# One core, a Flamingo block with a routed FFN: the streamed tile's three loads get a slot each on SP, and the slot tables of all engines are replaced

## What is computed

```
q = x @ Wq; k = ctx @ Wk                      # 4 heads of 32, 1024 context rows
scores = q k^T / sqrt(32)
topv, topi = top_k(scores, 32); probs = softmax(topv)   # scattered back, mean over heads
c_t = attn_mean @ (ctx @ Wv)
x' = layernorm(x) * (1 + scale_in(c_t)) + shift_in(c_t)
y  = s4d(x')                                  # long convolution, by real FFTs of 1024 points
y  = y * (1 + scale_out(c_t)) + shift_out(c_t)
xt = x_text + y; xt = layernorm(xt + gelu(ln(xt) @ W1) @ W2)
x  = x + tanh(g) * xt
x  = x + tanh(g2) * (shared_swiglu(ln(x)) + routed_swiglu(ln(x)))   # top-1 of 8 experts, score a sigmoid
```

## Time and profile before

| what | value |
|---|---|
| median of 3 runs | 1906.59 us (1902.35 to 1912.98) |
| profiled execution, its own time | 1909.8 us |
| span of the profiled execution | 1907.9 us |
| before the first MAX8 | 67.7 us |
| frame 0 | 230.4 us |
| frames 1, 2, 3 (no streamed tiles) | 178.4, 181.1, 180.9 us |
| frames 4, 5, 6, 7 | 202.8, 196.7, 194.8, 183.2 us |
| last MAX8 unit to the first of the 18 last tiles | 176 us (1616 to 1792) |
| the last tiles | about 116 us |
| DVE busy | 1564.8 us, 82% |

### The profile page before, as it was taken

One profiled execution on the slowest core, in us unless ns is written; L12 is line 12 of the kernel. 1 busy time (PEld: TensorE's weight loads), 2 busy tenths in 40 slices (PEclk: granted clock), 3 DMA queues, 4 the chain that ended last, 5 costly groups with the idle time before them and its releaser, 6 DMA issues. The chain is left out here.

```text
span 1907.9 us, 20758 instructions
## 1 busy us (share of the span) xinstructions
PE 1402.2 (73%) x6301; PEld 999.9 (52%) x6301; DVE 1564.8 (82%) x2300; ACT 1039.2 (54%) x2110; POOL 1185.0 (62%) x1293
## 2 busy tenths in 40 slices
...
GB/s 229 53 3 14 20 16 50 23 17 45 50 12 17 56 39 12 25 48 111 89 45 67 116 50 28 78 111 61 23 84 69 66 17 50 140 241 86 73 48 25
DMA packets 99219, 114.77 MB, mean 60 GB/s; under 512 B 18786, under 2 KB 77930, under 8 KB 98964
## 3 DMA queue, kind: packets, MB, share of 16 engines
q1 hardware_dynamic: 86964, 98.87, 17.8%
...
## 5 line engine op out<-in xcount | busy, mean ns | idle before, releaser
L1307 DVE MAX8 R<-ZB 128x8 f32<-128x1024 f32 x384 | 471.0, 1227 | 11.9
L1310 DVE MATCH_REPLACE8 ZB<-R,ZB 128x1024 f32<-128x1024 f32 x384 | 464.1, 1209 | 0.0
L669 POOL TENSOR_TENSOR ZB<-ZB 128x1024 f32<-128x1024 f32 x96 | 231.3, 2409 | 150.7 <-ACT ZB L944 146.5
L947 ACT ACTIVATE R<-PS 128x256 f32<-128x256 f32 (+6 forms) x378 | 160.4, 455 | 187.5 <-PE PS L1877 59.8
L944 ACT ACTIVATE R<-R 128x32 f32<-128x32 f32 (+2 forms) x352 | 95.1, 272 | 291.1 <-DVE R L1307 236.7
L671 POOL TENSOR_TENSOR ZB<-ZB 128x1024 f32<-128x1024 f32 x96 | 227.2, 2367 | 7.5
L1604 PE MATMUL PS<-ZR 97*128 97x512 f32 x128 | 81.4, 636 | 148.1 <-ACT ZB L944 120.0
L1299 DVE MAX8 R<-PS 128x8 f32<-128x1024 f32 x128 | 156.4, 1222 | 4.1 <-PE PS L1605 4.1
L950 ACT ACTIVATE R<-R 128x1 f32<-128x1 f32 (+1 forms) x384 | 141.0, 391 | 27.8 <-POOL R L656 23.5
L1303 DVE MATCH_REPLACE8 ZB<-R,PS 128x1024 f32<-128x1024 f32 x128 | 155.4, 1214 | 0.0
L944 ACT ACTIVATE ZB<-ZB,R 128x1024 f32<-128x1024 f32 x128 | 146.1, 1141 | 14.2 <-DVE ZB L1310 14.1
...
## 6 DMA issues: line engine op xcount, KB each, us to landing
...
ZR<-ZR SPq DMA_DIRECT2D x192, 32.0 KB
...
```

The source lines that it names most:

```text
L669: pool.tensor_tensor(e, e, w, ALU.subtract).then_inc(s.g_att, 1)
L947: return act.activation(o, i, ACT.Copy, **k)
L1307: vec.max(ml[:, 8 * r:8 * r + 8], w).then_inc(s.v_tk, 1)
L1310: vec.match_replace(w, ml[:, 8 * r:8 * r + 8], w, NEG).then_inc(s.v_tk, 1)
```

## The change

`tiles` on SP used to yield once for a tile and now yields three times: before the rows' load, before gate and up, and before down. Other streams of SP can come between. The waits are as they were. All slot tables are replaced with other numbers (`POOL_*`, `ACT_*`, `DVE_*`, `PE_*`, `POST_AT`, `SP_*`); no instruction is added or taken away, apart from the activation-table loads, which follow from ACT's order. Lines after 582 are one or two higher in the changed kernel.

```
-SP_QUERY = (28.1, 29.7, 33.4, 34.3)
-SP_TILE = ((-1.9,), (-0.2,), (2.5,), (56.5,), (71.3,))
+SP_QUERY = (24, 24, 24, 30)
+SP_TILE = ((-9.4, -4.9, -2.9), (-2.9, -2.9, -0.2), (2.5, 8.3, 11), (46.7, 46.7, 77.1), (92.3, 93.8, 97))
...
-PE_TILE = ((18.7, 20.4, 20.8, 25.5), (26.2, 38.3, 40, 42.2), (50.4, 53.2, 53.4, 54.1), (99.3, 101.3, 102.2, 104.1), (104.9,
-           106.9, 112.3, 116.5))
+PE_TILE = ((17.9, 23.9, 23.9, 33.4), (37.3, 40.5, 46.1, 51.7), (51.7, 58, 58.4, 58.8), (85.3, 95, 103.5, 109.1), (109.1,
+           113.2, 114.9, 114.9))
...
                     sp.dma_start(txs[j % 2], xs_d[bass.ds(row, 128), :]).then_inc(s_txs[j % 2], 16)
+                    yield tile_slot(j, SP_TILE, 1)
                     if j:
                         on.wait_ge(*q_run("tile", j - 1, T_UP))
                     for lo, nm in ((0, "gate"), (1024, "up")):
...
+                    yield tile_slot(j, SP_TILE, 2)
                     if j:
                         on.wait_ge(*q_run("tile", j - 1, T_DOWN))
```

More of the change, by code:

```diff
@@ L120 @@
 FILM_IN, DFT, INV, FILM_OUT, TURN, UP, DOWN, TURN2, GATE, RANK, COUNT, SHARED, SH_DOWN, NQ = 0, 4, 8, 10, 14, 16, 24, 28, 30, 31, 32, 33, 41, 45
[L123 to L158, removed]
@@ L159 @@
-ACT_EXP = (11.4, 9.3, 16, 13, 9.6, 10.8, 5.8, 8.2, 13.4, 18.4, 10.8, 10.4, 12.8, 8.8, 14.4, 7.6)
-ACT_REST = (12.5, 12.7, 16.9, 13.9, 10.1, 10.8, 10.4, 8.2, 13.6, 18.4, 11, 10.8, 16.8, 9.4, 15.1, 7.6)
-PE_SCORES = (-0.5, -5.2, -4.8, -3.6, -10.3, -6.8, -6.5, -3.1, -10.3, -2.9, 4.3, 1.2, 2.5, -2.3, -2.3, 0.1)
-PE_TILE = ((18.7, 20.4, 20.8, 25.5), (26.2, 38.3, 40, 42.2), (50.4, 53.2, 53.4, 54.1), (99.3, 101.3, 102.2, 104.1), (104.9,
-           106.9, 112.3, 116.5))
-ACT_TILE = ((28.4, 32.5, 34.6), (37.6, 42.9, 51.3), (52.6, 54.2, 60.8), (96, 101.9, 107.8), (108, 120, 120.9))
@@ L165 @@
[L165 to L178, removed]
@@ L179 @@
-SP_QUERY = (28.1, 29.7, 33.4, 34.3)
-SP_KEYS = (8.8, 4.2, 1.9, 0.2)
-SP_INPUT = (-1.7, -0.3)
-SP_POST = (2.2, 99.6, 100.6, 100.6, 121.9)
-SP_TILE = ((-1.9,), (-0.2,), (2.5,), (56.5,), (71.3,))
+POOL_FILM_IN = (7.4, 7.4, 7.8, 9)
+POOL_FOLD = (10.7,)
+POOL_SPECTRUM = (13.5, 19, 19.4, 19.4)
+POOL_INV = (31.2, 31.2)
+POOL_FILM_OUT = (31.2, 31.5, 31.5, 31.5)
+POOL_ROOT = (40.4, 90.5, 107.2)
+POOL_RESIDUAL = (57, 67.7, 77, 88.8)
+POOL_OUT = (90.5, 90.5, 91.8, 93.8)
+POOL_ROUTE = (117.8, 120.5, 121.6)
@@ new lines @@
+POOL_SH = (133.3, 134, 134.2, 134.5)
+POOL_PREP = (-7.8, 57.5)
+POOL_LOW = (3.4, 11.3, 47.5)
+ACT_FILM_IN = (21.9, 22.8, 23.6, 23.8)
+ACT_INV = (43.6, 49.3)
+ACT_FILM_OUT = (50.9, 50.9, 54.7, 54.8)
+ACT_ROOT = (61.8, 103.1, 112.8)
+ACT_NORM = (63.5, 116.4)
+ACT_TURN = (63.5, 63.5)
+ACT_UP = (71.8, 77.1, 77.1, 77.7, 77.7, 85.9, 87.2, 87.4)
+ACT_DOWN = (92.7, 95, 95, 100.2)
+ACT_OUT = (104.8, 105.5, 106.6, 108.5)
+ACT_TURN2 = (120.8, 120.8)
+ACT_ROUTE = (126.8, 127.6)
+ACT_SILU = (126.8, 134)
+ACT_SH = (137.8, 138.7, 141.3, 145.2)
@@ new lines @@
+DVE_SPECTRUM = (29.3, 30.4, 32.3, 33.5)
+DVE_MOMENTS = (55.6, 98.6, 110.1)
+DVE_ROUTE = (118, 120.2)
+DVE_SH = (126.3, 130.1, 131, 132.3)
+ACT_PREP = (6.4, 10.9, 20.4)
+ACT_QUERY = (22.6, 23.2, 26.6)
+ACT_CONTEXT = (8.3, 48.8)
+ACT_KEY = (18.8, 53)
+ACT_FINISH = ((1.4, 2.2, 11, 18.2), (9.3, 11.8, 17.7, 29.9), (4, 8.4, 18.6, 36.2), (4.9, 4.9, 8, 15.5))
+POOL_SUM = (5.8, -1.1, -3.4, -4.7, -8.6, -0.7, 1.4, -2.2, -1.4, 0.6, 3.1, 2.2, 1.9, 8, 11.3, 4)
+ACT_MAX = (5.2, 6.1, 6.4, 3.1, 10, 7.3, 2.9, 11.8, 10.8, 14.2, 10.3, 11.1, 7.5, 4.2, 17, 9.3)
@@ new lines @@
+ACT_EXP = (11.1, 11.2, 11.1, 4.8, 11.3, 10.4, 12.7, 13.8, 15.1, 16.6, 10.7, 11.7, 9.8, 8.8, 17, 9.3)
+ACT_REST = (12.8, 11.2, 11.1, 10.7, 12, 10.4, 14.7, 13.8, 17.9, 16.9, 10.9, 12.1, 11.2, 12.7, 17, 11.6)
+PE_SCORES = (3.4, -3, -4.1, -9.6, -7.7, -1.6, -4.9, 1.5, -3.7, -1, 0.2, -0.8, -4.2, -6.2, -1.9, -1.2)
+PE_TILE = ((17.9, 23.9, 23.9, 33.4), (37.3, 40.5, 46.1, 51.7), (51.7, 58, 58.4, 58.8), (85.3, 95, 103.5, 109.1), (109.1,
+           113.2, 114.9, 114.9))
+ACT_TILE = ((19.4, 26.1, 35.4), (35.4, 41.6, 58.9), (59.6, 61.4, 66.2), (93.8, 100.4, 105.8), (108.1, 115.6, 121.3))
@@ new lines @@
+DVE_TILE = ((25.2,), (51,), (57.8,), (102.8,), (113.6,))
+POOL_TILE = ((29.3,), (47.7,), (79.2,), (119.7,), (139.7,))
+DVE_CHUNK = ((-24.9, -22.3), (-22.3, -17.5), (29.9, 34.3), (44.4, 45.6), (53.9, 54.7), (68, 70.9), (73.3, 74.3), (86.8, 88))
+POOL_CHUNK = ((-62.7, -45.4, -33.6, -27.6, -7), (-29.1, -1.9, 7.7, 10.9, 11.1), (7.9, 16.5, 18.8, 23.6, 23.6), (22.6, 23.6,
+              31, 40, 43.5), (31, 44.7, 44.7, 52.1, 53.7), (49.1, 56.1, 56.1, 61.4, 62.1), (60.2, 68, 68.5, 68.8, 71.7),
+              (68.5, 82.1, 83.2, 85.6, 85.6))
```

11 lines of the change are left out of this document (added).

## The result

The changed kernel takes 1896.48 us (median of 5; 1892.5 to 1898.18) against 1906.59: ratio 0.9941, 95% interval 0.9916 to 0.9966. That is faster, by 0.6%, and inside the range; but the forecast was 32 us and the gain is 10. The profiled execution has a span of 1894.6 us, against 1907.9.

The account below looks back on a forecast made before the run. DVE was taken to bound frames up to 3; in frames 4 to 7 it waits, chiefly for late queries and POOL's order. Terms 26 - 1 + 10 + 2 + 3 - 5 - 3 = 32 us gave 1875 us, range 1856 to 1901.

Parts of the forecast that it names:

- Part 1: Frames 4 to 6: queries sent ahead of the last tile's loads; 26 us gained, 1 us lost to late keys.
- the chain's 38.8 us: DVE's waits at frames' ends, in frames 4 to 7; forecast to fall to 12.4 us, a gain of 26.4.
- rival A: At the last tile, another wait replaces the queries' and 15 to 26 us come back: 1890 to 1901 us; chance 0.15.
- the cover: Time between the previous tile's down load and the keys' DMAs at the key copy; forecast only some 9 us.
- Part 2: Frame starts: POOL's scatter ahead of both sums cuts DVE's 12.6 us of waits; 10 us gained, bounds 8.4 and 12.6.
- Part 3: Transform and moments: POOL earlier, first DOWN matmuls behind the transform's; 2 us gained, bounds 0 and 6.6.
- Part 4: After the attention: the scatter fills 2 us and the first DOWN moves; 3 us gained, bounds -2 and 5.
- Part 5: Every frame's end: ACT's softmax of unit 14 behind two SiLUs; costs 5 us, between 0 and 14.
- rival C: Frame ends: late shared-expert matmuls delay softmax, sum and scores; 1916 to 1930 us; chance 0.13 with other slower ways.
- D: Rival at ACT's frame ends: a table switch costs double its 1.28 us, adding 9 us: 1884; chance 0.05.
- Part 6: All else, including frames 0 to 3 and setup: small new waits cost 3 us, between 0 and 10.
- The worst case of the sum: Whole kernel, all terms at their worst: 5 us gained, 1902 us.

Follow-up runs that it names:

- SP's part alone: The kernel before with only the three yields on SP and the changed kernel's five SP tables; 1886.3 us, ratio 0.9854.
- the scatter's place alone: The kernel before with only POOL's scatter moved ahead of the sums of units 14 and 15; 1917.22 us, ratio 1.0031.
- the softmax's old place: The changed kernel with ACT's softmax of unit 14 back ahead of two SiLUs: 1896.53 us; with the eight matmuls too: 1872.81 us.
- the eight matmuls: The changed kernel with eight extra PE matmuls ahead of the second pair of turns in batches 0 to 2; 1879.29 us, again 1884.08.

## Why the prediction was right and wrong

*Part 1, the queries: right.* The 21.3 us for the SiLU are gone with SP's part alone, and of the chain's 38.8 us 13.9 stayed against the 12.4 forecast; of the ranks' 9.7 us, 7.6 are among them (below). The DMAs stand 113.3 us into frame 4, the key copy does not wait for them, and SP's part alone is worth 16 to 40 us by its interval, 28 at its middle, against the 26 taken. In frames 4 to 7 nothing took its place, so rival A did not come: SP issued the last tile's down load at 1010.52 and the keys from 1019.66, so the cover was 9 us, as said.

*Part 2, the scatter: the wait went, the gain is not shown.* The 12.6 us fell to 1.1. But the scatter's place alone costs time; I take it that it needs the router two DVE instructions earlier, which I had named as an addition to the gain. And with the waits for sums gone, frames 4 to 7 of the whole change are still only 1.4 us shorter than with SP's part alone (748.3 against 749.7): the waits for the ranks took their place.

*Part 3, transform and moments: wrong sign.* 2 us gained was the forecast; the waits at 1441 and 1443 are 5.2 + 3.9 and 0.8 + 1.9 = 11.8 us after, against 3.9 + 1.9 = 5.8 before, a loss of 6; the 2.7 us for the moments went.

*Part 4, after the attention: 4.4 us* against 3.

*Part 5, ACT at the frame's end: nothing in its own chain* (waits for sums 1.1 us), so neither rival C nor D came. Frames 1 to 3 did grow, which I had called the sign of C, but by the router's waits. The table load is again 1.28 us here, and the next ACTIVATE starts 0.01 us behind it (1021.07 and 1022.36). The 11 us that the softmax's old place gives with the eight matmuls are another mechanism.

*Part 6, all else: the step that failed.* "I put small new waits of this kind at 3 us, between 0 and 10", and frames 1 to 3 were to stay within 2 us. They lost 7 to 8 us each, 21.8 in sum. 14.0 + 3.3 = 17.3 us of this are the ranks and the gate, which ran at 1.2 GHz in place of 2.4. With the clock held up by eight matmuls, in the same order, DVE's idle time there is 9.1 us in place of 26.8, 17.7 less; the remaining 3.7 us over the kernel before are the rest. I had read PE's durations from the trace as if they belonged to the instructions. The trace of before had the warning in it: in frame 4 the same rank matmuls took 5.98 us and DVE's wait for them was 4.9 us, its longest in the earlier trace rows (the others are 1.1 and 2.6); I put all of it down to the late queries. SP's part alone left 7.6 of these 9.7 us in frames 4 to 7 (1.1, 1.1, 2.7 and 2.8 us). So the step that failed is a term for new waits of 3 us, at most 10, with no clock in it; the runs showed 17.3 us of slow router in frames 1 to 3 alone.

By the forecast's own sum: 26 - 1 + 10 + 2 + 3 - 5 - 3 = 32. The worst case of the sum took 3 us for the keys where part 1 allows 3 in each of three frames, 9; with that it ends 1 us slower than before and not 5 faster. With what was measured: frames 4 to 7 gave 32.3, the end 4.4, the start 0.8, frame 0 took 2.4 and frames 1 to 3 took 21.8: 13.3 us of span.
